# Routed experts in pairs and single row tiles, and a new order in three loops of a transformer kernel

## What is computed

```python
scores = jax.nn.sigmoid(flat @ centroids.T) + bias
vals, idx = jax.lax.top_k(scores, KR)            # KR = 4 of 16
gating = jnp.zeros_like(scores).at[jnp.arange(T)[:, None], idx].set(vals)
gating = gating / jnp.clip(gating.sum(-1, keepdims=True), 1e-08)
def step(acc, ew):
    w1, b1, w2, b2, g = ew                       # w1 512 x 352, w2 352 x 512
    hj = jax.nn.relu(flat @ w1 + b1)
    yj = hj @ w2 + b2
    return (acc + yj * g[:, None], None)
```

```python
scores = q_sem . k_sem2 / sqrt(32) + q_geo . k_geo2 / sqrt(32)   # scaled by exp(logit_scale)
scores = jnp.where(k_pos <= pos, scores, NEG_INF)
probs = jax.nn.softmax(scores, axis=-1)
out = probs @ v2, then @ Wo
```

## Time and profile before

| | us |
|---|---|
| median of 3 runs (lowest, highest) | 2113.64 (2112.92, 2113.86) |
| the profiled execution, its own time | 2117.64 |
| its span in the trace | 2115.8 |
| PE busy | 1791.7 (85%) |
| DVE busy | 1228.9 (58%) |
| POOL busy | 1033.7 (49%) |
| ACT busy | 830.0 (39%) |

### The profile page before, as it was taken

How to read it: one execution, slowest core, us unless ns; L and a number is a source line. 1 busy time by engine, 2 the same in 40 slices (tenths; PEclk the granted TensorE clock), 3 DMA queues, 4 the chain that set the end, 5 groups by cost and what they waited for, 6 DMA issues and landing times. The chain is left out here.

```text
span 2115.8 us, 27097 instructions
## 1 busy us (share of the span) xinstructions
PE 1791.7 (85%) x8864; PEld 1412.2 (67%) x8864; DVE 1228.9 (58%) x1820; ACT 830.0 (39%) x1330; POOL 1033.7 (49%) x654
## 2 busy tenths in 40 slices
PE   3299999999999688896479955866999999996996
PEld 2178888888888333342248844655999999995775
DVE  5244545454445488989516523662566666665886
ACT  3233333333332345554232212453666666651121
POOL 0325454545453254455222555214787877754564
PEclk7699999999999899998779976887999999998998
DMA  5533333323233401122580151003888887876564
GB/s 207 207 120 120 103 119 100 123 91 131 90 124 131 155 20 60 63 97 79 196 299 1 51 183 51 1 1 132 281 283 278 281 285 278 281 225 223 179 205 134
DMA packets 106853, 316.80 MB, mean 150 GB/s; under 512 B 14530, under 2 KB 16160, under 8 KB 105504
## 3 DMA queue, kind: packets, MB, share of 16 engines
q1 hardware_dynamic: 89536, 266.07, 36.8%
q0 software_dynamic: 17248, 49.86, 7.0%
HBM read 248.17 MB, written 67.71 MB: 149 GB/s over the span
## 5 line engine op out<-in xcount | busy, mean ns | idle before, releaser
L704 DVE TENSOR_TENSOR rows<-rffn_ps_y,rows 128x512 f32<-128x512 f32 x255 | 172.9, 690 | 126.2 <-PE rffn_ps_y L790 124.1
L630 POOL TENSOR_TENSOR rffn_w0l<-rffn_raw,rffn_w0h 128x1536 fp32r<-128x1536 f32 x15 | 52.7, 3511 | 154.3 <-ACT rffn_w0h L651 154.3
L723 DVE TENSOR_TENSOR rffn_ps_h<-rffn_ps_up,rffn_silu 128x512 f32<-128x512 f32 (+1 forms) x80 | 47.4, 593 | 124.3 <-PE rffn_ps_up L767 124.0
L1905 POOL DMA_INDIRECT moe_x_in<-xn_rows,moe_idx_now x94 | 97.7, 1040 | 21.2 <-issue 14.7
L1911 POOL TENSOR_TENSOR moe_w_0l<-moe_raw,moe_w_0h 128x1536 fp32r<-128x1536 f32 x24 | 84.4, 3515 | 38.5 <-ACT moe_w_0h L1936 38.5
L1911 POOL TENSOR_TENSOR moe_w_1l<-moe_raw,moe_w_1h 128x1536 fp32r<-128x1536 f32 x23 | 80.9, 3516 | 33.1 <-ACT moe_w_1h L1936 33.1
L1978 DVE COPY moe_y<-moe_ps_y 128x512 f32<-128x512 f32 x94 | 64.3, 686 | 51.7 <-PE moe_ps_y L2019 48.7
L677 ACT CAST rffn_hT0h<-rffn_ps_h 128x512 fp32r<-128x512 f32 (+1 forms) x48 | 24.8, 516 | 155.8 <-DVE rffn_ps_h L723 141.1
L2935 POOL DMA_INDIRECT att_rows<-ys,pos x64 | 65.9, 1030 | 40.0 <-POOLq L55 23.1
L630 POOL TENSOR_TENSOR rffn_w4l<-rffn_raw,rffn_w4h 128x1536 fp32r<-128x1536 f32 x16 | 56.1, 3507 | 59.6 <-ACT rffn_w4h L651 59.6
L1985 DVE TENSOR_TENSOR moe_w_0l<-moe_raw,moe_w_0h 128x1536 fp32r<-128x1536 f32 x24 | 59.0, 2457 | 43.2 <-ACT moe_w_0h L1950 43.2
(11 more groups left out here) (716 smaller groups left out, 6260.9 us busy)
## 6 DMA issues: line engine op xcount, KB each, us to landing
rffn_raw<-in_ffn_w SPq DMA_DIRECT2D x80, 768.0 KB, 4.3
moe_raw<-in_moe_w SPq DMA_DIRECT2D x47, 769.5 KB
moe_raw<-in_moe_w SPq DMA_DIRECT2D x47, 768.0 KB, 4.6
ys<-moe_y SPq DMA_DIRECT2D x47, 512.0 KB
xs<-route_zero SPq DMA_DIRECT2D x17, 256.0 KB
rffn_x_in<-xs SPq DMA_DIRECT2D x17, 256.0 KB, 2.8
ys<-rows SPq DMA_DIRECT2D x17, 256.0 KB, 2.1
rows<-in_x SPq DMA_DIRECT2D x4, 1024.0 KB
```

Source lines behind the costliest of these rows:

```text
L630: nc.gpsimd.tensor_tensor(w[b][LO][:], raw[m % 2][:], f32(w[b][HI][:]), ALU.subtract).then_inc(s_w, 1)
L704: nc.vector.tensor_tensor(y[:, t, :], yb[g % 2][:], y[:, t, :], ALU.add).then_inc(s_yadd, 1)
L723: nc.vector.tensor_tensor(hp[:, cols], ub[n % 2][:, cols], sil[n % 2][:, cols], ALU.mult)\
L1905: nc.gpsimd.indirect_dma_start(out=x_in[j][tt][:], out_offset=None, in_=xn_dram, in_offset=bass.IndirectOffsetOnAxis(ap=now[j][:, tt:tt + ...
```

## The change

**Experts.** The rows of an expert are laid out in pairs of tiles of 128 rows and, where a last tile is odd, in a single one: 31 pairs and 17 singles, 48 units, 79 tiles of 128 rows in place of 94. Their order is fixed (`MKINDS`: pair, pair, single fourteen times, then pair, single three times), and the hardware loop makes six units a turn (`MCYC`), with six ahead and twelve behind written out. `raw2` is doubled, so w2 is loaded two units ahead, before the w2 of the next unit is used; `xs` is single; `h32` is gone, relu writes back to its PSUM bank and the casts read there. PE's hidden matmuls therefore wait for the low part of h of the unit before, which is later than its relu. POOL gathers unit m + 2 before it splits w1 of unit m + 1. On ACT and DVE the work on h and on the next x is interleaved. The PSUM banks of x and y alternate by tile (`bank`).

**Router.** It finds the odd last tile of each expert (`odd`, `odd_upto`, `ends`, `jump`) and moves the places of its rows behind the pairs; the chain for `keep.expert` finds the experts of pairs and singles apart.

**Window and attention.** Calls change places.

```diff
-            link(nc.vector.tensor_tensor(more, cum[:, :, NT - 1:NT].to_broadcast([P, E, 8]),
-                                         starts.unsqueeze(1).to_broadcast([P, E, 8]), ALU.is_gt))
-            link(nc.vector.tensor_reduce(tiles[:], more, AX.X, ALU.add))
+            link(nc.vector.tensor_tensor(more, cum[:, :, NT - 1:NT].to_broadcast([P, E, 16]),
+                                         starts.unsqueeze(1).to_broadcast([P, E, 16]), ALU.is_gt))
+            link(nc.vector.tensor_reduce(tiles[:], more[:, :, 0:8], AX.X, ALU.add))
+            link(nc.vector.tensor_reduce(odd[:], more[:, :, 8:16], AX.X, ALU.add))
+            link(nc.vector.tensor_tensor(odd[:], odd[:], tiles[:], ALU.subtract))
             link(nc.vector.tensor_tensor_scan(upto[:], ones[:, 0:E], tiles[:], 0.0, ALU.mult, ALU.add))
+            link(nc.vector.tensor_tensor_scan(odd_upto[:], ones[:, 0:E], odd[:], 0.0, ALU.mult, ALU.add))
             link(nc.vector.tensor_tensor(base[:], upto[:], tiles[:], ALU.subtract))
             link(nc.vector.tensor_scalar(base[:], base[:], float(MR), -1.0, ALU.mult, ALU.add))
+            link(nc.vector.tensor_scalar(ends[:], upto[:], float(MR), None, ALU.mult))
...
+            link(nc.vector.tensor_tensor(jump[:], odd_upto[:], odd[:], ALU.subtract))
+            link(nc.vector.tensor_scalar(jump[:], jump[:], -float(P), float(P * (MG - 1)), ALU.mult, ALU.add))
+            link(nc.vector.tensor_tensor(jump[:], jump[:], ends[:], ALU.subtract))
             link(nc.vector.tensor_tensor(cum, cum, total, ALU.subtract))
             link(nc.vector.tensor_tensor(cum, cum, base[:].unsqueeze(2).to_broadcast([P, E, NT]), ALU.add))
             link(nc.vector.tensor_tensor(place, counts[:, 0], cum.rearrange("p e t -> p t e"), ALU.add))
+            link(nc.vector.tensor_tensor(prod, place, ends[:].unsqueeze(1).to_broadcast([P, NT, E]), ALU.is_ge))
+            link(nc.vector.tensor_tensor(prod, prod, jump[:].unsqueeze(1).to_broadcast([P, NT, E]), ALU.mult))
+            link(nc.vector.tensor_tensor(place, place, prod, ALU.add))
...
-MT = T * 4 // MR + 15
+MP, MS = 31, 17
+MU = MP + MS
+MG = 2 * MP + MS
 MF = 3
+
+
+MKINDS = [2, 2, 1] * 14 + [2, 1] * 3
+MCYC = 6
...
-        raw2 = a.sb("raw2", [P, W2])
+        raw2 = [a.sb(f"raw2_{j}", [P, W2]) for j in range(2)]
...
-        xs = [[a.sb(f"xs{j}{'hl'[s]}", [P, KC, MR], F32R) for s in (HI, LO)] for j in range(2)]
-        h32 = [a.sb(f"h32_{f}", [P, MR]) for f in range(MF)]
...
+            for m in range(MCYC):
+                run(0, m)
+            with eng.Fori(1, MU // MCYC - 2) as i:
+                for m in range(MCYC):
+                    run(i, m)
+            for m in range(2 * MCYC):
+                run(MU // MCYC - 2, m)
...
-            def run(s, j):
-                if after(s, 2):
-                    src = weights_of(A["moe_w1"], s + 2)
-                    wait(sp, s_w1, s + 1)
-                    sp.dma_start(raw1[j][:], src).then_inc(s_raw1[j], 16)
-                if after(s, 1):
-                    src = weights_of(A["moe_w2"], s + 1)
-                    wait(sp, s_w2, s + 1)
-                    sp.dma_start(raw2[:], src).then_inc(s_raw2, 16)
-                if not (isinstance(s, int) and s == 0):
-                    store(s - 1)
...
+            def run(i, m):
+                if exists(i, m + 2):
+                    src = weights_of(A["moe_w1"], i, m + 2)
+                    wait(sp, s_w1, number(i, m) + 1)
+                    sp.dma_start(raw1[m % 2][:], src).then_inc(s_raw1[m % 2], 16)
+                if exists(i, m + 2):
+                    src = weights_of(A["moe_w2"], i, m + 2)
+                    wait(sp, s_w2, number(i, m) + 1)
+                    sp.dma_start(raw2[m % 2][:], src).then_inc(s_raw2[m % 2], 16)
+                if not at_start(i, m):
+                    store(i, m - 1)
...
-            def run(s, j):
-                if after(s, 1):
-                    split(s + 1, 1 - j)
-                if after(s, 2):
-                    gather(s + 2, j)
-            tiles(pool, run)
+            def run(i, m):
+                if exists(i, m + 2):
+                    gather(i, m + 2)
+                if exists(i, m + 1):
+                    split(i, m + 1)
...
-                for f in range(MF):
+            def run(i, m):
+                j, n, s = m % 2, kind(i, m) * P, number(i, m)
+                if exists(i, m + 1):
+                    split1(i, m + 1)
+                wait(act, s_raw2[j], 16 * (MCYC // 2 * i + m // 2 + 1))
+                if not at_start(i, m):
+                    wait(act, s_y, tiles_ahead(i, m - 1))
+                nc.scalar.copy(w2[j][HI][:], raw2[j][:]).then_inc(s_w2hi, 1)
+                def relu(f):
                     wait(act, s_hid, MF * s + f + 1)
-                    wait(act, s_h, MF * (s - 1) + f + 1)
                     if f == 0:
                         wait(act, s_b1, s + 1)
-                    nc.scalar.activation(h32[f][:], hb[f][:], ACT.Relu, bias=b1[j][:, f:f + 1]).then_inc(s_h32, 1)
-                for f in range(MF):
+                    nc.scalar.activation(hb[f][:, 0:n], hb[f][:, 0:n], ACT.Relu, bias=b1[j][:, f:f + 1]).then_inc(s_h32, 1)
+
+                def high_h(f):
                     wait(act, s_h32, MF * s + f + 1)
-                    nc.scalar.copy(h[j][HI][:, f, :], h32[f][:]).then_inc(s_hhi, 1)
-                if after(s, 1):
-                    high_x(s + 1, 1 - j)
-            tiles(act, run)
+                    nc.scalar.copy(h[j][HI][:, f, 0:n], hb[f][:, 0:n]).then_inc(s_hhi, 1)
+                relu(0)
+                relu(1)
+                high_h(0)
+                relu(2)
+                high_h(1)
+                if exists(i, m + 1):
+                    high_x(i, m + 1)
+                high_h(2)
...
+                def low_h(f):
                     wait(dve, s_hhi, MF * s + f + 1)
-                    nc.vector.tensor_tensor(h[j][LO][:, f, :], h32[f][:], f32(h[j][HI][:, f, :]), ALU.subtract)\
+                    nc.vector.tensor_tensor(h[j][LO][:, f, 0:n], hb[f][:, 0:n], f32(h[j][HI][:, f, 0:n]), ALU.subtract)\
                       .then_inc(s_h, 1)
-                if after(s, 1):
-                    low_x(s + 1, 1 - j)
-                if not (isinstance(s, int) and s == 0):
-                    copy_y(s - 1)
-            tiles(dve, run)
-            copy_y(MT - 1)
+                low_h(0)
+                low_h(1)
+                if exists(i, m + 1):
+                    low_x(i, m + 1)
+                low_h(2)
+                if not at_start(i, m):
+                    copy_y(i, m - 1)
...
-                    wait(pe, s_h32, MF * (s - 1) + f + 1)
+                    wait(pe, s_h, MF * (s - 1) + f + 1)
...
-                            last = nc.tensor.matmul(hb[f][:], w1[j][p][:, col:col + P], xs[j][q][:, c, :],
+                            last = nc.tensor.matmul(hb[f][:, 0:cols], w1[j][p][:, col:col + P], xs[q][:, c, 0:cols],
...
+            exps(0)
             for u in range(2 * HKV):
-                exps(u)
-                if u:
-                    probs_high(u - 1)
                 probs(u)
+                if u + 1 < 2 * HKV:
+                    exps(u + 1)
+                probs_high(u)
                 if u >= 3 and u % 2:
                     out_high((u - 3) // 2)
-            probs_high(2 * HKV - 1)
...
+            shift(0)
             for u in range(2 * HKV):
-                shift(u)
+                inverse(u)
+                if u + 1 < 2 * HKV:
+                    shift(u + 1)
                 if u:
                     probs_low(u - 1)
-                inverse(u)
...
-                turn(u)
                 if u + 2 < 2 * HKV:
                     scores(u + 2)
+                turn(u)
...
+            def geo_scores(i):
+                out = sb_[i % 2]
...
+                if 0 <= n - 1 < NR:
+                    scores(n - 1)
                 if 0 <= n - 2 < NR:
                     turn_p(n - 2)
                 if 0 <= n - 1 < NR:
-                    scores(n - 1)
+                    geo_scores(n - 1)
```

235 lines of the change are left out of this document (136 added, 99 removed).

## The result

The changed kernel takes 2089.45 us (median, 2088.56 to 2092.0), the kernel before 2113.75 in the same comparison (2112.92 to 2117.04): a ratio of 0.9884, 95% interval 0.9867 to 0.9901, so 24 us or 1.2% faster. Predicted were 2066, with a range from 2048 to 2090. The direction held and the time lies at the slow edge of the range, half a microsecond inside it; only half of the forecast gain came.

A forecast was written before the change was run, and what follows sets the result against it. PE bound the experts (busy 414.17 of 414.60 us), rings of engines the other three changed places. Experts -31, router +3, window -6, attention -13 make -47: 2117.6 to 2070.6, less 4.0: 2066, range 2048 to 2090.

The forecast's parts named there:

- Rivals 1 and 2: Experts' units bound by weights or POOL, 10 to 15 lost, chance .16; reordered loops give nothing, 10 to 19 lost, .12.
- PE's own work in the experts, -37.2: Experts: 31 pairs at 9.32 us and 17 singles at 6.58 make 400.8 in place of 438.0, 37.2 less.
- Third rival: Experts, singles: 128-column matmuls cost .059 to .085 in place of .112, -16 to -32 us; chance .06.
- Waits of 5 us in the experts: Experts: tightest units and load jitter cost 5 us of waits in 48 units, bounds 0 and 25.
- H + 15.5: Experts' weight ring: from hidden start H through low_x takes 15.5 us, against two PE units; tightest slack .4.
- Rival 1: Experts: units bound by weights or POOL, average unit from 8.35 to 8.65 us, total 2076 to 2085; chance .16.
- Rival 5: Experts: w1 load behind the store in SyncE's queue makes units average over 9.46 us, from 2114 up; chance .03.
- Gather ahead of the split, put at nothing: Experts, POOL: w1 split up to 4.4 us later but covered, 22.6 a cycle against PE's 25.2.
- Start-up +1: Experts' start: 1 us for the fourth .77 MB load ahead of the first gathered rows.
- Router +3: Router: links added on DVE's row ahead of the first positions shift POOL's scatters; +3 us (2 to 4.5).
- Window -6: Window loop: DVE's period falls from 7.18 to 5.2 to 5.6, out_low waits eat half; -6 us (-9 to -1).
- Attention -13: Attention: folded matmuls ahead of turn_p fill PE's waits; 3.7 + 2.9 + 3 + 4 given as -13 (-17 to -7).

The follow-up runs named there:

- w1_first: Changed kernel with SyncE's w1 load of unit m + 3 issued ahead of the store of unit m - 1: 2073.35 us, ratio 0.9814.
- before_w1_first: Kernel before with SyncE's w1 load of tile s + 3 ahead of the store of tile s - 1: 2118.06 us, ratio 1.0011.
- split_behind: Changed kernel with DVE's split of w2 behind low_h and low_x in place of ahead of them: 2090.85 us, ratio 0.9888.
- both: Changed kernel with the w1 load ahead of the store and the w2 split behind low_x: 2077.69 us, ratio 0.9835.
- gather_behind: Changed kernel with POOL's old order, split of w1 ahead of the gather: 2096.63 us, ratio 0.9929.
- late_w2: w1_first with the w2 load of unit 1 issued behind the first turned rows, not ahead of the gathers: 2078.19 us, ratio 0.9824.

## Why the prediction held in direction and missed half the gain

That the time lies within the range is partly luck. Rivals 1 and 2 were each priced alone, and what came is the first and nearly half of the second together: the experts lost 12 more than allowed, the two loops 8 of their 19. The median lies half a microsecond inside the range, while the four times it is taken from lie 3.4 apart and the slowest, 2092.0, is outside. The parts of the sum, one by one:

- **PE's own work in the experts, -37.2: right.** With the waits gone the stage is 409.4 against 446.1, -36.7. Third rival out: 128 columns are spaced .110. The 81 ns that the prediction quotes from the Trainium skill (TensorE: Matmul & The Clock Gate, Back-to-back issue gap) are not borne out by any row here.
- **Waits of 5 us in the experts: the step that failed, 17.3 in its place.** "H + 15.5" walked the ring of the weights from the load through the casts of ACT straight to relu, high_x and low_x, and left out DVE's split of w2, which stands in DVE's queue ahead of low_h and low_x and which the change left in its place. And it took 5.95 from issue to use from one row; in the case above it is 7.4, and ACT has w1 at H + 9.9 in place of H + 8.3. These two, 1.8 and 1.6, turn H + 15.5 into about H + 18.9, an estimate; low_x ends at 1552.44, H + 18.5, and PE's two units take 15.9 to 18.0. Rival 1 says this, and its price (10 to 15) holds the 12 more than allowed that were lost. The walk could have been tried on the trace of before: there low_x of the same unit as in the earlier trace rows ends at H + 17.2 and not by H + 15.5, behind a split of 2.70 and a relu that waited .79 for PE:

```profile
1730.03 2.70 DVE L1985 TENSOR_TENSOR moe_w_0l<-moe_raw,moe_w_0h 128x1536 fp32r<-128x1536 f32 x1 [2.14 <-ACT moe_w_0h L1950]
...
1733.66 1.27 DVE L1970 TENSOR_TENSOR moe_xs1l<-moe_ps_x,moe_xs1h 128x512 fp32r<-128x512 f32 x2
```

The runs show that the first link to loosen is the issue of w1 behind the store (w1_first, before_w1_first), not the split (split_behind, both). Rival 5, the slower one, named this very queue as its place, and was right in that; its price fell short of the point from which it decides (a mean unit of 9.46; it was about 8.7).
- **The clock behind a wait** was in no term: .71 for 5.9 us after 2.2 us of waiting. The waits in the stage are 15.7 us, of which 2.1 are left in w1_first; the other 3.7 of the 17.3 are this clock and what the views do not name.
- **Gather ahead of the split, put at nothing:** by gather_behind it saves 6 us or more, so without it the waits would have been longer still.
- **Start-up +1:** +2.0, of which late_w2 shows 1.2 for the fourth load. The rest is no more than two profiles differ: with the experts of before the stretch takes 26.4, 25.6 and 27.5.
- **Router +3: right,** 3.1 us of chain, and POOL's wait ahead of its first scatter is 8.03 where it was 4.91.
- **Window -6: mechanism right, size -3.5.** The 1.99 of idle time is gone and maxima come every 5.11 us as long as no out_low stands between them, a little faster than walked. But out_low waits 3.77, 6.23 and 5.87 at its three places, 15.9 together, where I had taken 4 three times:

```profile
1379.79 1.22 DVE L2718 TENSOR_REDUCE win_mw<-win_ps_q 128x4 f32<-128x1024 f32 x1
...
1384.90 1.22 DVE L2718 TENSOR_REDUCE win_mw<-win_ps_q 128x4 f32<-128x1024 f32 x1
...
1391.81 0.69 DVE L2762 TENSOR_TENSOR win_qTl<-win_ps_scores,win_qTh 128x512 fp32r<-128x512 f32 x1 [3.77 <-ACT win_qTh L2634]
...
1408.95 0.69 DVE L2762 TENSOR_TENSOR win_qTl<-win_ps_scores,win_qTh 128x512 fp32r<-128x512 f32 x1 [6.23 <-ACT win_qTh L2634]
```

- **Attention -13: size wrong, -7.6.** (The four terms of the prediction make 13.6, not 13.) First period -2.5 (forecast 3.7), second -2.1 (2.9), the steady ones -2.4 (3), the last -.6 (4). At both ends the folded part fills the wait as forecast, but the geometric part then meets a wait that I had not looked for: `att_qTl`, which DVE makes behind the softmax.

```profile
1920.31 0.66 PE L3195 MATMUL att_ps_pT<-att_ident,att_p 128*128 128x128 f32 x4 [3.40 <-DVE att_p L3108]
...
1922.23 0.47 PE L3217 MATMUL att_ps_scores<-kqh,att_qTh 128*128 128x128 f32 x1 [1.27 <-DVE att_qTl L3161]
```

In the steady periods the bound has changed engine. DVE's 1.3 of waiting for the scores is gone, and the period fell only from 11.58 to 11.48, since DVE's own work grew: over five periods it is busy 55.07 of 57.38 us with the same 81 instructions that took 49.12 of 57.91 before. The growth is in one operation, the scaling of the probabilities, about 2.17 us where it was .93, since it now falls together with the whole of an addition of POOL (5 times 1.24 is 6.2, the growth 5.95):

```profile
1982.84:2040.22 57.38, 55.86 (x285) 45.87 (x285) 55.07 (x81) 12.20 (x20) 32.86 (x31) 1.00 0.68 206
```

```profile
1988.45 2.17 DVE L3108 TENSOR_TENSOR att_p<-att_p,att_inv 128x512 f32<-128x512 f32 x1
1988.76 1.30 POOL L3040 TENSOR_TENSOR att_res<-att_res,att_x_in 128x512 f32<-128x512 f32 x1
```

That the overlap is the cause can be read within the traces. In after, the first and the last of the 14 scalings meet no addition and take .69; one that meets the last .37 us of the addition takes .93, as in the steady periods of before; eleven meet 1.21 to 1.31 us of it and take 1.77 to 2.18. Wherever they meet, the scaling ends about .56 us after the addition does:

```profile
1919.56 0.69 DVE L3108 TENSOR_TENSOR att_p<-att_p,att_inv 128x512 f32<-128x512 f32 x1
...
2015.58 1.31 POOL L2948 TENSOR_TENSOR att_res<-att_res,att_x_in 128x512 f32<-128x512 f32 x1
...
2016.52 0.93 DVE L3016 TENSOR_TENSOR att_p<-att_p,att_inv 128x512 f32<-128x512 f32 x1
```

The last two rows are of before. In old_attention, where only the order of the attention loop is taken back, none is longer than .93 again. No run moved the addition by itself, so what a freed addition would bring is not shown.
